# Scattering edge rows in two parts, so that the attention layer starts on the first while GpSimd still sends the second; place sums on ScalarE

## What is computed

```python
edge_index = stack([src, dst])
h = maximum(layernorm(x), 0)
x = x + L0(h)       # GCN: h @ W_lin @ W_gcn, deg over dst, norm = dinv[src] * dinv[dst],
                    # out = segment_sum(h[src] * norm, dst) + b_gcn; layernorm, gamma, beta, relu
h = maximum(layernorm(x), 0)
x = x + L1(h)       # attention of 4 heads over the edges, grouped by src:
                    # q = h @ Wq + bq; k = edge_attr @ Wk + bk; v = edge_attr_n2 @ Wv + bv
                    # score = (q[src] . k) * scale per head; softmax over the edges of one src
                    # out = segment_sum(attn * v, src) @ Wo + bo
```

## Time and profile before

| | |
|---|---|
| median of 3 runs | 4944.86 us (4943.92 to 4951.8) |
| profiled execution: time, span | 4901.44 us, 4899.7 us |
| mean granted TensorE clock | 0.774 |
| busy: TensorE, VectorE, ScalarE, GpSimd | 3393.7 us (69%), 3287.0 us (67%), 1581.0 us (32%), 2004.0 us (41%) |
| DMA | 750.98 MB, mean 153 GB/s |
| layer-1 groups | 588, 408.0 KB and 64.5 KB each |

### The profile page before, as it was taken

How to read it: one execution, slowest core, us unless ns; L and a number is a source line. 1 busy time by engine, 2 the same in 40 slices (tenths; PEclk the granted TensorE clock), 3 DMA queues, 4 the chain that set the end, 5 groups by cost and what they waited for, 6 DMA issues and landing times. The chain is left out here.

```text
span 4899.7 us, 77060 instructions
## 1 busy us (share of the span) xinstructions
PE 3393.7 (69%) x21063; PEld 2364.7 (48%) x21063; DVE 3287.0 (67%) x5668; ACT 1581.0 (32%) x4329; POOL 2004.0 (41%) x1688
## 2 busy tenths in 40 slices
PE   3358846566666566666651555699999999999898
PEld 2146623333333333333330333477777777777665
DVE  7778877777777777777767000477777777777611
ACT  0011122222222222222220332466666666666411
POOL 2887788777777777777770000100000000000000
PEclk8555557787778878878775555799999999999855
DMA  2554445555555555555551111466666666666400
GB/s 87 181 170 167 153 156 178 179 183 187 179 181 179 180 189 179 180 181 182 186 178 38 31 34 32 123 189 190 190 188 191 186 190 190 188 190 186 135 0 26
DMA packets 499583, 750.98 MB, mean 153 GB/s; under 512 B 53384, under 2 KB 368624, under 8 KB 499438
## 3 DMA queue, kind: packets, MB, share of 16 engines
q1 hardware_dynamic: 394878, 509.78, 34.9%
q0 software_dynamic: 78160, 226.14, 12.3%
q10 hardware_dynamic: 26400, 13.21, 0.9%
HBM read 506.87 MB, written 242.05 MB: 153 GB/s over the span
## 5 line engine op out<-in xcount | busy, mean ns | idle before, releaser
L628 POOL DMA_INDIRECT table_s<-ring,place x1612 | 1935.0, 1200 | 516.4 <-issue 479.2
L904 PE MATMUL bank<-xres 128*128 128x98 bf16 x3136 | 345.3, 263 | 743.4 <-DVE xres L778 476.5
L663 DVE TENSOR_REDUCE place<-row_base 128x8 int32<-128x1568 f32 x202 | 360.8, 1786 | 491.8 <-DMA table_s<-ring,place 488.1
L593 ACT CAST work<-bank 128x392 bf16<-128x392 f32 x784 | 373.4, 506 | 964.6 <-PE bank L904 504.1
L904 PEld LDWEIGHTS bank<-xres 128*128 128x128 bf16 x3136 | 262.9, 159 | 861.4 <-DVE xres L778 521.7
L923 PE MATMUL bank<-parts,work 128*128 128x384 bf16 x2401 | 618.8, 428 | 0.2 <-issue 0.2
L1281 PE MATMUL bank<-kT,G 128*128 128x384 f32 x1176 | 511.9, 517 | 0.2 <-ACT kT L1328 0.2
L1301 PE MATMUL bank<-kv_rows,exT 128*128 128x129 f32 x3528 | 493.8, 276 | 0.0
L1301 PEld LDWEIGHTS bank<-kv_rows,exT 128*128 128x128 f32 x3528 | 443.5, 193 | 0.1
L1372 DVE TENSOR_REDUCE gmax<-bank 128x1 f32<-128x384 f32 x588 | 326.4, 555 | 157.1 <-PE bank L1281 112.2
L923 PEld LDWEIGHTS bank<-parts,work 128*128 128x128 bf16 x2401 | 295.3, 127 | 258.7 <-issue 197.4
(11 more groups left out here) (264 smaller groups left out, 4405.5 us busy)
## 6 DMA issues: line engine op xcount, KB each, us to landing
kv_rows<-table_s SPq DMA_DIRECT2D x588, 408.0 KB, 3.1
ring<-in_kv SPq DMA_DIRECT2D x402, 512.0 KB
G<-G_dram SPq DMA_DIRECT2D x588, 64.5 KB, 2.7
table_s<-ring,place POOLq DMA_INDIRECT x1612
G_dram<-gst ACTq DMA_DIRECT2D x50, 258.0 KB, 3.0
out<-xres SPq DMA_DIRECT2D x1, 3072.0 KB
raw_src<-in_src SPq DMA_DIRECT2D x1, 805.5 KB
parts<-in_dst SPq DMA_DIRECT2D x1, 805.5 KB
```

What stands on the lines that cost most here:

```text
L593: nc.scalar.copy(m["blocks"][:, t % 2, :, at:at + 4 * GN].rearrange("p h (g w) -> p g h w", w=GN), m["bank"][4 + e % 2][:, 0:4 * GW].rearr ...
L628: pool.indirect_dma_start(out=m["table_s"], out_offset=bass.IndirectOffsetOnAxis(ap=m["place"][0:n, u, k:k + 1], axis=0), in_=m["ring"][0: ...
L663: dve.tensor_reduce(m["place"][:, i % KRING, :], m["products"][:, :].rearrange("p (s t) -> p s t", t=STILES), AX_X, ALU.add).then_inc(m["p ...
L904: last = pe.matmul(m["bank"][4 + e % 2][:, g * GW:(g + 1) * GW], m["hot_l"][:, k, :, x * 4 + g], m["hot_w"][:, k, x * 4 + g, :], start=(g ...
```

## The change

The edges are sorted in two parts. The first is ranking steps 0 to 135 of every stream, 139264 edges; the second is the rest, 66986. Each part has its own counts, bases, padding and group list, and its own stretch of `table_s`. Layer 1 takes 396 groups of the first part, then 204 of the second, each part padded to whole groups of a tile.

GpSimd sends 132 of the 202 steps in the sorting block, 24 in the node block and 46 in layer 1. So all `place` values are kept (`[P, STEPS, STREAMS]`), and ranking doesn't wait for a slot. SP loads the rows for the steps in layer 1 between its group loads, one step after every six groups. GpSimd copies the source number into the rows itself, out of a kept array `sources`. The sum over tiles goes from one reduction on VectorE to eight activations with accumulated output on ScalarE; for that the product is made in two halves, and the one-hot lies with the stream innermost against a ruler that is written out. Gathers of keys have four slots instead of two and are asked for earlier. The ring stays allocated in layer 1; `xres` is stored to HBM in the node block and loaded back into the ring's place (`x_again`) after the last row is sent. The weight products move from the sorting block to the front block.

```diff
-HALF_NGS = NGS // 2
+FIRST_STEPS = 136
+PART_EDGES = (FIRST_STEPS * STREAMS * P, E - FIRST_STEPS * STREAMS * P)
+PART_ROWS = (0, PART_EDGES[0] + SGE)
+PART_ENDS = (PART_EDGES[0], E + SGE)
+PART_GROUPS = tuple(groups(e, STILES, SGE, SRING) for e in PART_EDGES)
+PART_USUAL = (396, 204)
+NGS, USUAL = sum(PART_GROUPS), sum(PART_USUAL)
+POOL_STEPS = (132, 156)
+KEY_RING = 4
...
+def load_rows(m, sp, i):
+    rows, u = m["kv"][0:P * W, :].rearrange("(p j) w -> p j w", j=W), i % KRING
+    need(sp, m["rows_sent"][u], sent_before(i))
...
+def scatter_rows(m, pool, i):
+    u, first = i % KRING, STREAMS - columns(i)
+    need(pool, m["rows_sent"][u], sent_before(i))
+    pool.tensor_copy(m["ring"][:, u, first:STREAMS, KEY_AT:KEY_AT + 1], m["sources"][:, i, first:STREAMS].rearrange("p (s a) -> p s a", a=1)).then_inc(m["keys_ready"], 1)
+    pool.wait_ge(m["places_ready"], i + 1)
+    pool.wait_ge(m["rows_loaded"][u], 32 * (i // KRING + 1))
+    pool.wait_ge(m["keys_ready"], i + 1)
+    for k in range(first, STREAMS):
+        n = TAIL if i == STEPS - 1 and k == STREAMS - 1 else P
+        pool.indirect_dma_start(out=m["table_s"], out_offset=bass.IndirectOffsetOnAxis(ap=m["place"][0:n, i, k:k + 1], axis=0),
+                                in_=m["ring"][0:n, u, k, :], in_offset=None).then_inc(m["rows_sent"][u], 16)
...
-    SORT_LISTS, LN, DEGREES, DEG_RATE, FEATURES = 6, 8, 15, 4, 16
+    SORT_LISTS, LN, DEGREES, DEG_RATE, FEATURES = 6, 9, 16, 4, 17
...
-        gathers.setdefault(max(FIRST_HOT - 3, key_step(b) - 6), []).append(b)
+        gathers.setdefault(max(FIRST_HOT - 4, key_step(b) - 16) * POOL_STEPS[0] // STEPS, []).append(b)
...
+            def sums(i):
+                for h in range(2):
+                    act.wait_ge(m["selected"], 2 * i + h + 1)
+                    for k in range(STREAMS // 2):
+                        at = m["products"][:, h, :, k:k + 1].rearrange("p t a -> p (t a)")
+                        last = nc.scalar.activation(at, at, ACT.Identity, accum_out=m["place_f"][:, i % 2, h * STREAMS // 2 + k:h * STREAMS // 2 + k + 1])
+                    last.then_inc(m["half_summed"], 1)
+                act.wait_ge(m["half_summed"], 2 * i + 2)
+                nc.scalar.copy(m["place"][:, i, :], m["place_f"][:, i % 2, :]).then_inc(m["places_ready"], 1)
...
             def hot(i):
                 need(dve, m["counted"], i - 1)
-                dve.tensor_tensor(m["among"][:, i % 2, :].rearrange("p (s t) -> p s t", t=STILES), row_of(m["ruler"][:, :], [P, STREAMS, STILES]),
-                                  column(m["keys_t"][:, i, :], [P, STREAMS, STILES]), ALU.is_equal).then_inc(m["hot_ready"], 1)
+                dve.tensor_tensor(m["among"][:, i % 2, :].rearrange("p (t s) -> p t s", s=STREAMS), m["ruler"][:, :, :],
+                                  row_of(m["keys_t"][:, i, :], [P, STILES, STREAMS]), ALU.is_equal).then_inc(m["hot_ready"], 1)
...
-                need(dve, m["places_ready"], i)
                 dve.wait_ge(m["ranked"], i + 1)
...
-                need(dve, m["rows_sent"][i % KRING], sent_before[i])
-                dve.wait_ge(m["selected"], i + 1)
...
+                for h in range(2):
+                    at = slice(h * STREAMS // 2, (h + 1) * STREAMS // 2)
+                    need(dve, m["half_summed"], 2 * i - 1 + h)
+                    dve.tensor_tensor(m["products"][:, h, :, :].rearrange("p (b t) s -> p b t s", b=RANK_BANKS),
...
             def rank(i):
+                if i == FIRST_STEPS:
+                    pe.wait_ge(m["selected"], 2 * i)
+                    for b in range(RANK_BANKS):
+                        one = slice(P // RANK_BANKS * b, P // RANK_BANKS * b + 1)
+                        pe.matmul(m["banks"][:, b, 0:LANES_BANK], m["ones"][one, :], m["second_row"][one, :], start=True, stop=True)
... nodes_block
             pool.memset(m["xres"][:, N // P:NT, :], 0.0).then_inc(m["x_padded"], 1)
+            for i in range(*POOL_STEPS):
+                scatter_rows(m, pool, i)
...
             load_x(m, sp)
+            for i in range(POOL_STEPS[0] + KRING, POOL_STEPS[1] + KRING):
+                load_rows(m, sp, i)
+            sp.wait_ge(m["x_ready"], 1)
+            sp.dma_start(node_tiles(m["x_dram"]), m["xres"][:, :, :]).then_inc(m["x_stored"], 16)
+            sp.wait_ge(m["x_stored"], 16)
... layer1_block
+                for u in range(KRING):
+                    sp.wait_ge(m["rows_sent"][u], sent_before(FIRST_STEPS + (u - FIRST_STEPS) % KRING))
+                second = PART_USUAL[0] // SRING
+                for r in range(second):
+                    for u in range(SRING):
+                        body(r * SRING + u, u, r)
+                    if POOL_STEPS[1] + KRING + r < STEPS:
+                        load_rows(m, sp, POOL_STEPS[1] + KRING + r)
+                for i in range(STEPS, STEPS + KRING):
+                    sp.wait_ge(m["rows_sent"][i % KRING], sent_before(i))
+                sp.dma_start(m["x_again"][:, :, :], node_tiles(m["x_dram"])).then_inc(m["x_reloaded"], 16)
+                steps(sp, body, second, last, SRING)
...
             pool.memset(m["agg"][:, :, :], 0.0).then_inc(m["rows_ready"], 1)
+            for i in range(POOL_STEPS[1], STEPS):
+                scatter_rows(m, pool, i)
```

More of the change, by code:

```diff
@@ L54, with groups @@
 VW = D + 1
-def groups(tiles, slots, ring):
-    n = -(-(E + tiles * (slots - 1)) // slots)
+def groups(edges, tiles, slots, ring):
+    n = -(-(edges + tiles * (slots - 1)) // slots)
     return n + -n % ring
[L63 to L67, removed]
+NGD = groups(E, TILES, GE, RING)
 PAD_KEY = P * P - 1
@@ L355, in source_counts, with counts @@
     dve.wait_ge(m["src_counted"], 1)
[L356 to L366, removed]
+    n = STILES
+    def counts(part, q):
+        return m["bank"][part * half + q // 2][:, q % 2 * HIS * LOS:q % 2 * HIS * LOS + n]
+    for part, base in enumerate((m["row_base"], m["second_base"])):
+        total, start, end = (m[t][:, part, :] for t in ("cnt_s", "start_s", "end_s"))
+        c(dve.memset(base[:, 0, :], 0.0))
+        for q in range(STREAMS):
+            c(dve.tensor_tensor(base[:, q + 1, :] if q < STREAMS - 1 else total, base[:, q, :], counts(part, q), ALU.add))
+        c(dve.memset(end, 0.0))
+        c(dve.tensor_tensor_scan(start, total, end, 0.0, ALU.add, ALU.add))
+        c(dve.tensor_tensor(start, start, total, ALU.subtract))
+        if part:
+            c(dve.tensor_scalar(start, start, float(PART_ROWS[1]), None, ALU.add))
+        last = c(dve.tensor_tensor(base[:, :, :], base[:, :, :], row_of(start, [P, STREAMS, n]), ALU.add))
+    tiles = LANES_BANK // STREAMS
+    for b in range(RANK_BANKS):
+        one = slice(P // RANK_BANKS * b, P // RANK_BANKS * b + 1)
+        last = dve.tensor_copy(m["second_row"][one, :].rearrange("p (t s) -> p t s", s=STREAMS), m["second_base"][one, :, b * tiles:(b + 1) * tiles].rearrange("p s t -> p t s"))
+    last.then_inc(m["row_base_ready"], 1)
 def count_sources(nc, m, pe):
@@ L457, in scatter_block @@
     FIRST_HOT = STARTS + 3
-    def columns(i):
-        return STREAMS if i < STEPS - 1 else STREAMS - SHORT
-    def slots(i):
-        return range(STREAMS - columns(i), STREAMS)
     def share(i, first, end, n):
@@ L600, in _ @@
                     evacuate(j)
-                keys(i)
-                weights(i)
+                sums(i)
                 if i == LN + 6:
```

408 lines of the change are left out of this document (221 added, 187 removed).

## The result

The changed kernel takes 4898.85 us (median of 4 runs, 4883.61 to 4900.89); the kernel before, run beside it, 4945.86 us (4943.92 to 4951.8). The ratio is 0.9896, 95% interval 0.9874 to 0.9918: 1% faster, where 10.5% was forecast.

The account below looks back on a forecast made before the run. The prediction took GpSimd's indirect DMAs to bound ranking in the sorting block, with everybody else waiting. Its terms, -602 + 7 + 31 + 10 + 40 = -514, scaled to -519, gave about 4425 us, range 4280 to 4620.

Parts of the forecast that it names:

- GpSimd's wait before its first gather: Sorting block: after 29 steps GpSimd must wait for `starts_ready`, about 600 us, losing 80 us.
- ranking ends the block: Rival, sorting block: ScalarE's sums of 0.71 us make ranking finish last, at 2072 us; time 4505 us, chance 0.17.
- TensorE stays at 1.2 GHz: Rival, sorting block: TensorE's clock stays low, ranking steps take 9.9 to 10.2 us, time 4680 us; chance 0.04.
- sums over 0.7 us: Sorting block: sign that would prove the forecast wrong, ScalarE's sums longer than the 0.58 us assumed.
- the first rival: Sorting block: ScalarE's sums at 0.71 us make ranking end the block, 9.1 us a step, time 4505 us; chance 0.17.
- GpSimd's 24 steps lie inside 500: Node block: GpSimd's 24 steps, 324 us (367 at most), fit within the block's 500 us.
- +7 of `bo`: Node block: adding `bo` ahead of the 50 iterations brings 6.83 us of hidden work onto the path.
- +31 for more groups: Layer 1: 600 groups instead of 588, at 2.62 us each, add 31 us.
- +10 for the clearing of `agg`: Layer 1: GpSimd first clears `agg` (21.17 us), stopping row loads from group 6 on, 10 us once.
- +40 for full transfers: Layer 1: DMA full at 16.1 us of work in 15.5, costing 40 us, bounds 0 and 103.
- layer 1 runs into the transfers, 103 us or more: Rival, layer 1: transfers cost 103 us or more, the rest as forecast; time 4490 to 4550 us, chance 0.1.
- GpSimd's 13.5 is under 15.5, so not again: Layer 1: GpSimd's 13.5 us a step fits in six groups' 15.5 us, so row loads stall only once.

Follow-up runs that it names:

- e2: Changed kernel with GpSimd's late sends kept but no row loads after the sorting block, so old ring contents are sent: 4858.64 us.
- e3: Changed kernel with late rows loaded and stored by SP's plain DMAs, GpSimd idle after step 135, second part reading first-part rows: 4792.71 us.
- e5: Changed kernel with the node block's 50 iterations written out on TensorE, ScalarE and VectorE instead of a hardware loop: ratio 0.9857 to the kernel before.
- e12: Changed kernel with all products of the node block in bf16 (results rounded): 4710.5 us, loop 367.9 us.
- e9: Changed kernel with a GpSimd memset of 256 elements behind each send after the sorting block: 4564.11 us, ratio 0.9184 to the kernel before.
- e14: Changed kernel with a one-element GpSimd memset behind each late send: 4812.93 us, node loop 457.7 us.
- e16: Changed kernel with a GpSimd memset of 128 elements behind each late send: 4473.21 us, node loop 372.2 us.
- e1: Changed kernel with no row loaded or sent after the sorting block; layer 1's second part reads rows of the first: 4432.06 us.
- e13: Changed kernel with paced late sends (one per group in layer 1), row loads in pieces, 124/32 sorting/node steps, later gathers: 4314.3 us, ratio 0.878 to before.
- e8: Changed kernel, late rows stored by SP's plain DMAs without GpSimd, layer 1's row loads only into slots stored a round earlier: 4669.28 us.

## Why the prediction was wrong

Where the profiled time went, term by term (us):

| term | forecast | measured |
|---|---|---|
| ranking starts | 116 | 123.5 |
| 43 steps done | 587 | 594.7 |
| last place | 1888 (587 + 1280 + 21) | 1891.4 |
| GpSimd's wait before its first gather | 80 | 85.8 |
| GpSimd, a step | 13.5 | 13.7 (824 sends from 599 to 2006) |
| sorting block | -602 | -587 |
| node block | +7 | +164 |
| layer 1 | +81 | +423 |
| output block | 0 | -4 |
| sum | -514 | -4 |

**The sorting block was right**, mechanism and sizes: GpSimd ended it, after the ranking, and the wait stands in the profile as forecast.

```profile
POOL key_rows L696 <- DVE starts L793: 85.8, 1, 85.8
```

The rivals "ranking ends the block", "TensorE stays at 1.2 GHz" (granted 0.87) and "sums over 0.7 us" (0.54) are refuted by it. Three sums of the prediction are slightly off, without effect on this: the first 16 steps' terms give 119 us, not 125; the upper bound of a sum gives 0.73 us, not 0.71; and the first rival's terms give 4515, not 4505.

**The step that failed first** is "GpSimd's 24 steps lie inside 500": that work which fits beside a block costs it nothing. They did fit, sent by about 2340 us, but 1.265 us a send is a pace that holds up TensorE, and the loop took 523.0 us instead of 374.1. e2, e3, e5 and e12 rule out the traffic alone, the hardware loop and the data type; e9, e14 and e16 show that it is the spacing of the sends. The forecast took GpSimd's 13.5 us a step from stretches in which VectorE's comparisons lengthen every few sends; with VectorE idle a step took 10.85 us. The block's +7 of `bo` was right: from the block's start to the first `hs` 105.3 us pass instead of 98.5.

**In layer 1** the +31 for more groups holds: the groups after the 396th take 516.5 us in e1 and 486.8 in the kernel before, +30. The +10 for the clearing of `agg` can't be read there. e1 has no row loads for it to hold up, and its first twelve groups take 30.1 us, before 30.6. The wait of 10 us that every changed run has instead, at the reload of x, is a term that the forecast put at nothing; that the sum of the two comes to e1's +42 is luck. In the changed kernel the first twelve groups took 67.8 us, because GpSimd then sends the four steps that lie loaded, 32 sends, without a pause. The +40 for full transfers holds roughly, once nothing else interferes: e13 moves the late rows beside the groups and takes 50.5 us more than e1 in them.

```profile
2437.00:3510.00 1073.00, 942.97 (x6713) 749.33 (x6712) 793.68 (x2769) 615.24 (x1584) 377.61 (x408) 0.97 0.87 269
```

DMA share 0.87 here, near the 0.9 that the forecast gave, though with 269 GB/s and not 323, against 0.64 in the changed kernel (2710 to 3500 us). So the rival "layer 1 runs into the transfers, 103 us or more" named the right block and the wrong mechanism: the DMA engines were not full. What failed is "GpSimd's 13.5 is under 15.5, so not again". GpSimd kept up easily and waited for loads, 550.2 us of 1000:

```profile
POOL table_s L550 <- DMA ring<-in_kv: 550.2, 40, 20.3
```

But it then sent the eight DMAs of a step in one run at 1.265 us. Counted over 43 steps from 2700 to 3700 us, TensorE starts 4.1 to 6.8 products per us up to the fifth send of such a run, 1.2 between the fifth and the sixth, and 0.3 to 0.4 up to the eighth; in e2 the fall comes at the fourth, in e16 there is none below 3.8. Of 385 us, this alone makes 332 (e2), and 266 go when the gap alone is added (e16). The rest is the 1 MB loads, which overlap with it: behind one, `kv_rows` lands after 5.8 us in the median, past its 5.3 us of lead.

**What stays open** is where in the chip the products are held. In the node block they are rationed by number; in layer 1 the hold-up begins at the fourth or fifth send of a run at 1.265 us; at 1.35 us neither is seen. No run shows what they wait for. Every run had its clock and spans recorded, so none shows whether it is so without recording. In the sorting block of the kernel before TensorE also starts fewer products late in such runs, but there VectorE waits too, and the two can't be separated.

## What to carry over

Work that is moved beside another block must be priced at the pace it will have there, not at the pace it had beside its old neighbours: an engine that was slowed by VectorE runs free, and its burst can hold up others even where no compute engine is busy all the time and the DMA share is 0.6. Give such background work a pace tied to the foreground (one send and a quarter of a load per group, not eight and 1 MB per six), and check how much lead each foreground load has, since a burst in its queue comes out of that lead. Test the overlap with the work taken out, then with its traffic alone and with its instructions alone, before trusting a sum of busy times.

## What the runs showed of the hardware

- GpSimd's indirect DMAs of 128 rows of 1088 bytes at one every 1.265 us cut TensorE to one product instruction per 1.8 us in the node block (133 float32 and 132 bf16 in 240 us); at 1.35 us they cost its loop nothing (372.2 us). The Trainium skill (SBUF — State Buffer, Who interferes with whom) says that DMA never contends with a compute engine. For plain DMAs the trace agrees (e3: share 0.82, loop 372.5 us); for GpSimd's sends in close order the measurement says otherwise (523.0 us), whatever the path is.
- A useless memset of 0.33 us behind each late send made the whole kernel 7% faster (e9's ratio to before 0.9184 instead of 0.9896).
- In SP's queue a load of 408 KB lands after 3.1 us by itself, after 5.8 us behind 1 MB (changed kernel) and after 7.9 us behind 2 MB (e8).
- ScalarE's sum over 196 elements takes 0.54 us from start to start: the read-out starts 0.45 us behind its `ACTIVATE`, the next `ACTIVATE` 0.09 us behind that (changed kernel, 1600 to 1606 us).
